# Delta rule: a head's outputs are computed behind the next head's key products, its query products become fillers of the first two levels, and values are projected first

## The reference, cut to what matters

```python
mixed = causal_conv4(hidden @ qkv_w.T)            # 4 taps per channel
q, k, v = split(mixed, 3)                         # 8 heads of 128 each
z = hidden @ z_w.T
beta = sigmoid(hidden @ b_w.T)
alpha = exp(-exp(A_log) * softplus(hidden @ a_w.T + dt_bias))
def step(S, q_t, k_t, v_t, beta_t, alpha_t):      # over the 256 tokens
    S = S * alpha_t
    kv = k_t @ S
    S = S + outer(k_t, (v_t - kv) * beta_t)
    return S, q_t @ S
o = scan(step)
o = o * rsqrt(mean(o * o) + eps) * norm_w         # per head
out = (o * silu(z)) @ out_w.T                     # summed over heads
```

## Time and profile before

| | us |
|---|---|
| median of 3 runs | 4471.35 (4461.21 to 4476.52) |
| the profiled execution | 4470.14 |
| its span (first to last instruction) | 4468.4 |
| of it, heads 1 to 6 of the delta rule | 591.40 |
| PE busy in these | 533.42 |
| DVE, ACT, POOL busy in these | 326.79, 253.91, 147.82 |

### The profile page before, as it was taken

How to read it: one execution, slowest core, us unless ns; L and a number is a source line. 1 busy time by engine, 2 the same in 40 slices (tenths; PEclk the granted TensorE clock), 3 DMA queues, 4 the chain that set the end, 5 groups by cost and what they waited for, 6 DMA issues and landing times. The chain is left out here.

```text
span 4468.4 us, 119856 instructions
## 1 busy us (share of the span) xinstructions
PE 3704.9 (83%) x48264; PEld 2804.5 (63%) x48456; DVE 2663.5 (60%) x4159; ACT 2214.2 (50%) x4350; POOL 1676.8 (38%) x1564
## 2 busy tenths in 40 slices
PE   4666759989989989988988986999999765667998
PEld 1223448868868868867867874666667752225555
DVE  5985567547637727726736736455556255894554
ACT  4443247657647747746756753344444314441222
POOL 1652047527617707716725732222222202661000
PEclk7988979999999999999999997677778777997999
DMA  0000011101101101101101100000000000001000
GB/s 14 0 0 16 1 45 33 38 22 33 42 17 33 40 19 33 31 21 41 32 25 37 31 14 6 6 6 6 7 6 7 4 12 0 0 0 57 0 0 9
DMA packets 56555, 83.31 MB, mean 19 GB/s; under 512 B 13146, under 2 KB 32628, under 8 KB 54900
## 3 DMA queue, kind: packets, MB, share of 16 engines
q1 hardware_dynamic: 56052, 75.99, 5.7%
HBM read 30.87 MB, written 1.05 MB: 7 GB/s over the span
## 5 line engine op out<-in xcount | busy, mean ns | idle before, releaser
L1814 POOL TENSOR_TENSOR local_rot<-local_term 128x512 f32<-128x512 f32 x384 | 478.7, 1268 | 639.3 <-DVE local_term L2132 639.3
L2132 DVE TENSOR_TENSOR local_term<-bank,local_table 128x512 f32<-128x512 f32 x768 | 484.7, 673 | 107.2 <-ACT local_sq L2020 98.7
L2055 ACT ACTIVATE local_attn<-bank 64x256 f32<-64x256 f32 x768 | 290.8, 379 | 338.7 <-PE bank L1911 331.9
L272 POOL TENSOR_TENSOR mamba_hc<-mamba_state,mamba_c_all 128x512 f32<-128x512 f32 x256 | 319.6, 1270 | 318.0 <-DVE mamba_state L451 311.5
L1820 POOL TENSOR_TENSOR local_rot<-local_rot,local_inv 128x512 f32<-128x512 f32 x384 | 392.4, 1043 | 92.5 <-ACT local_inv L2031 91.1
L1855 PE MATMUL bank<-local_w_layer,local_xs 128*128 128x256 f32 x1536 | 400.8, 406 | 24.8 <-issue 17.7
L1855 PEld LDWEIGHTS bank<-local_w_layer,local_xs 128*128 128x128 f32 x1536 | 287.8, 197 | 78.5 <-issue 28.4
L2193 DVE TENSOR_REDUCE local_most<-bank 128x8 f32<-128x512 f32 x192 | 132.8, 692 | 307.8 <-PE bank L1890 307.8
L1911 PE MATMUL bank<-local_pt,local_v_moved 64*128 64x64 f32 x3072 | 314.3, 282 | 0.0
L1911 PE MATMUL bank<-local_pt,local_v_at 64*128 64x64 f32 x3072 | 305.2, 276 | 0.0
L451 DVE TENSOR_TENSOR_SCAN mamba_state<-bank,mamba_dbu 128x512 f32<-128x512 f32 x256 | 297.9, 1203 | 0.0
(11 more groups left out here) (367 smaller groups left out, 8268.7 us busy)
## 6 DMA issues: line engine op xcount, KB each, us to landing
local_v_moved<-local_v_at SPq DMA_DIRECT2D x192, 192.0 KB, 2.4
local_w_layer<-a_w_layer_dram SPq DMA_DIRECT2D x6, 1536.0 KB, 7.3
local_v_moved<-local_v_at SPq DMA_DIRECT2D x192, 32.0 KB, 2.0
moe_w<-f_w_dram SPq DMA_DIRECT2D x3, 2048.0 KB, 15.8
local_w_o<-a_w_o_dram SPq DMA_DIRECT2D x12, 256.0 KB, 3.7
local_w_up<-a_w_up_dram SPq DMA_DIRECT2D x6, 341.0 KB, 4.2
moe_w<-f_w_dram SPq DMA_DIRECT2D x3, 576.0 KB, 5.2
delta_w_h<-g_w_qkv_dram SPq DMA_DIRECT2D x8, 192.0 KB, 2.2
```

The source lines that it names most:

```text
L272: ins = pool.tensor_tensor(hc[:, b, h, :], state[:, b, h, :], c_all[:, b, :], ALU.mult)
L1814: pool.tensor_tensor(rot[:, i % 2, :, f, :], here[:, :, f, :], there[:, :, 1 - f, :], ALU.add).then_inc(summed, 1)
L2055: ins = act.activation(tokens[ch, v, :, :].rearrange("p k (r q) -> p k r q", r=2), g.bank[6 + v][ch, :].rearrange("p (k r h q) -> p k r h ...
L2132: dve.tensor_tensor(term[:, which, b, :], g.bank[b][:, :], table[:, which, :, :].rearrange("p n c -> p (n c)"), ALU.mult).then_inc(roped, 1)
```

## The change

- The output products of head h leave the end of head h. Three quads stand in head h+1 behind its key products and between its first products, the fourth in slot 0 (letter u). Only head 7's stand behind its own head.
- Their squares (ACT), sums (DVE), logarithm, exponential and scaling move with them (letter n, slot 1).
- The query products leave the front of the head for slots 2 to 5 (letter q), with their multiplication on DVE.
- Values are turned in slots 1 to 3, keys in slots 4 and 5, two quads at once, in banks 2 and 3.
- Projections come two slots later at first (p0 in slot 6, before in slot 4), and in the order values, keys, queries.
- `w_sol` gets a buffer of its own, as `lt` is written anew while the outputs are still to be computed.

```diff
-    PROJ, STEPS, ORDER = 3 * GROUPS, TAPS - 1, (1, 0, 2)
+    PROJ, STEPS, ORDER = 3 * GROUPS, TAPS - 1, (2, 1, 0)
...
-        w_sol, o_sq, sz = lt, o_t, g.xn
+        w_sol = sb("w_sol", [P, QUADS, QUAD, C])
+        o_sq, sz = o_t, g.xn
...
-        AT_SLOT = {0: "v0 v1", 1: "k0 k1", 2: "v2 v3", 3: "k2 k3", 4: "p0", 5: "a0", 6: "p1", 7: "a1", 8: "p2", 9: "a2",
+        AT_SLOT = {0: "u3", 1: "v0 v1 n0", 2: "q0 v2", 3: "q1 v3", 4: "q2 k0", 5: "q3 k1", 6: "p0", 7: "a0 p1", 8: "p2",
...
+                if later(h):
+                    pool.wait_ge(o_ready, h * QUADS)
...
+            def weigh_output(h, n):
+                if n == 0:
+                    pe.wait_ge(sz_ready, h * QUADS + QUADS)
+                pe.wait_ge(w_copied, h * (2 * QUADS) + (QUADS + n + 1))
+                for i in range(QUAD):
+                    mm = pe.matmul(chunk(g.bank[4 + n], i), at[:, n, i, :], w_sol[:, n, i, :], start=True, stop=(i < SEQS))
+                    if i >= SEQS:
+                        mm = pe.matmul(chunk(g.bank[4 + n], i), kq_g[:, 0, SEQS * n + i - SEQS, :], s_one[:, n, i - SEQS, :],
+                                       start=False, stop=True)
+                mm.then_inc(o_ready, 1)
...
-                pe.wait_ge(conv_step, h * (PROJ * STEPS) + GROUPS * STEPS)
+                pe.wait_ge(conv_step, h * (PROJ * STEPS) + 2 * GROUPS * STEPS)
                 for n in range(QUADS):
+                    if later(h):
+                        pe.wait_ge(w_copied, h * (2 * QUADS) - (QUADS - 1 - n))
                     four(g.bank[n], lambda i: seg(1, n, i), lambda i: seg(1, n, i), kk_ready)
-                pe.wait_ge(conv_step, h * (PROJ * STEPS) + PROJ * STEPS)
                 pe.wait_ge(a_copied, h * QUADS + QUADS)
-                queries_by_keys(0)
-                queries_by_keys(1)
+                if later(h):
+                    pe.wait_ge(conv_step, h * (PROJ * STEPS) + PROJ * STEPS)
+                    weigh_output(h - 1, 0)
                 first_products(0)
-                queries_by_keys(2)
+                if later(h):
+                    weigh_output(h - 1, 1)
                 first_products(1)
-                queries_by_keys(3)
+                if later(h):
+                    weigh_output(h - 1, 2)
...
+                    if later(h) and hf == 0:
+                        square_output(h - 1, 0)
+                if later(h):
+                    square_output(h - 1, 1)
+                    square_output(h - 1, 2)
```

## The result

The changed kernel takes 4512.81 us (median of 4 runs, 4509.47 to 4525.85) against 4467.19 for the kernel before in the same comparison: a ratio of 1.0101 (95% interval 1.0077 to 1.0126). It is slower by 45.6 us in the medians (45 by the ratio) and by 39.3 in the two profiled executions (4509.47 and 4470.14). The forecast was 4498.

A forecast was written before the change was run, and what follows sets the result against it. PE was taken as the bound: its work at the granted clock plus pauses, a 256-instruction packet taking at least 3.8 us. 4470.1 + 20.5 (five branch-entered heads at +4.1) - 4.5 + 12 = 4498; range 4450 to 4522.

The forecast's parts named there:

- Branch, +3.2: Loop branch into heads 2 to 6: PE waits for two instruction packets, idle 4.8 against 1.6 us, +3.2 each.
- Tail, -5.1: End of a head: output products leave, one projection comes later, a turned output earlier; other waits unchanged; -5.1 us.
- Front, +6.0: Start of heads entered by the branch: +3.6 us with waits for POOL and q0, 2.4 for key products' clock.
- Clock in the levels, +12: Levels: packets with two projections exceed 3.8 us at half clock; +2 us a head, +12 in all.
- Others, -4.5: Heads entered without the branch: heads 1 and 7 -1.5 us each, head 0 -1.5 from two query quads leaving.
- A: Rival: the packet boundary behind the branch costs nothing, idle stays 1.6, clock isn't lost; 4470 us, chance 0.20.
- B: Rival: output and query products keep the clock at 1.0 through the levels; faster, 4446 us, chance 0.17.
- C: Rival: clock falls at the branch, returns only in the last level; up to +9 a head, 4540 us, chance 0.09.

The follow-up runs named there:

- aligned_square: aligned with ACT's square of the first output quad moved behind the second packing instead of between the packings: 4471.9 us, ratio 1.0018.
- 161 and 250 left: Changed kernel padded with extra PE instructions so the loop body starts 161 or 250 instructions ahead of a packet boundary: 4486.1 and 4504.6 us.
- aligned: Changed kernel, loop body 161 instructions ahead of a packet boundary, extra instructions put where PE waits anyway: 4479.8 us, ratio 1.0035.
- b_left2: Kernel before, order untouched, padded so its loop body starts 2 instructions ahead of a boundary instead of 161: 4502.8 us, ratio 1.0093.
- a_left63: Changed kernel padded with extra PE instructions so the loop body starts 63 instructions ahead of a packet boundary: 4512.0 us, ratio 1.0103.
- aligned_order: aligned with padding spread, the square behind the second packing and the last two output projections each ahead of a projection in their slots: 4449.0 us, ratio 0.9971.

## Why the prediction was nearly right

**Branch, +3.2.** Right in kind: a target 2 instructions ahead of a boundary costs two packets, 3.0 apart, as in the earlier trace rows. Measured +4.0 a branch (5.6 instead of 1.6). I let the target's packet move 1.2 before PE is done, as before; in the change it moves 0.25 before. The last products now wait for DVE's last subtraction, and in all five heads the branch begins 0.16 after that has ended, so it comes up later.

**Tail, -5.1.** The work went, as computed. The sentence "the rest of the tail waits as before" is the step that failed. The two waits for DVE's add, 1.25 and 0.77 before (1.24 and 0.77 in the head shown), became one of 2.53, long enough for the clock to fall; with the clock, PE's work in last stretch and tail together falls by 1.0 a head instead of the 4.4 that left it (39 records fewer). Together the two stretches, without the branch, are 0.5 a head shorter, not 5.1. I had listed what moved on PE and not how long DVE needs to its add, and so not that PE's work beside it shrinks by half.

**Front, +6.0.** Measured: +3.6 up to the levels' first product, of it 1.0 for POOL (1.1 expected from ACT's square; in aligned_square this wait is gone) and 1.4 to 2.8 of the key products' clock (2.4 taken). The rest of the 6.0, such as q0's wait of 1.13 for ACT's scaling, doesn't show in the sum: front and levels together are 4.5 longer, and with the 2.0 for the clock I had given them 8.0.

**Clock in the levels, +12.** The levels are 0.9 a head longer, 4.9 over heads 1 to 6, although the clock in them is higher than before (0.74 on average, before 0.62). Another 1.3 a head is in the last stretch behind them, beyond the 2.5 of work that came there; its clock is 0.83 instead of 0.88. That the two add up to about 12 is luck. What I named beside the clock, two packets with two projections each, was a cost, and the runs show it as part of the 3.5 a head between 161 and 250 left.

**Others, -4.5.** Head 0 and the step to head 1 (from the first product with `delta_w_ab` to head 1's first key product) take 141.5 instead of 144.5, 3.0 less where I had computed 6.6. This can't be judged from single profiles: aligned and aligned_square run the same instructions there and take 130.4 and 139.4. The tail ahead of head 7, which has no branch, is 4.8 shorter. Heads 1 and 7 lose 3.4 and 3.8 in the last stretch, where I had counted none (2.5 of it in head 1 is work that came there from the tail).

**Rivals.** A (the boundary costs nothing) falls by b_left2 alone, which is slower with no change of order. B (fillers keep the clock up) had a true premise, the clock in the levels rose, and a price that did not come: the levels got longer, not shorter. The price was not baseless. In the kernel before, the levels of heads 1 to 6 last 53.4 at a clock of 0.56 and 48.8 at 0.65, so there the clock did matter, and the rest of the difference between the earlier trace rows's heads lies in the last stretch (16.6 to 20.0). C did not occur: the clock comes back within 3.4 to 6.8 us.

**The sum.** It came out 15 low (4498 against 4512.8) because large errors nearly cancel. Over heads 1 to 6 last stretch and tail cost some 28 more than forecast and the five branches 4, while front and levels cost 22 less. That leaves 9 of the 11 by which the profiled execution (4509.5) lies above the forecast. The branch, which decided between the forecast and its rivals, was understood; that the total is this near is in part luck.

## What to carry to other kernels

In a program that is bound by its instructions' arrival, shifting code moves every packet boundary behind it: count where a loop's target and the heavy instructions fall before you judge a new order, since here that was 29 to 40 of 45 us. If a wait is for an engine's small result, list what this engine has ahead of it and what the waiting engine has to do meanwhile, and look for the second waiter before moving it; a wait removed in one place came back 5 us later. A stretch whose length doesn't follow its work is the place for fillers, and the order paid (16 us below the kernel before) only once the tail kept its clock and the target its packet.

## What the runs showed of the hardware

- A met wait costs PE's queue 0.11 us an instruction: 97 of them 10.4 us, 159 17.4, 195 21.2, where 64 records of products of 32x32 take 0.74 together. As padding they belong where the engine waits anyway.
- The packets behind a branch overlap with work as soon as the first has something to run. With 63 instructions left, the packets moved at 3096.25 and 3099.25, and the 32 key products ran through from 3098.90 in 3.83 us without a stop; with 2 left nothing runs until 2.6 behind the second. By the Trainium skill, page "Runtime: NRT & Kernel Launch", section "Instruction fetch mechanics", crossing a block is mostly hidden; that agrees with 63, 161 and 250 left behind the branch (idle once, 2.4 to 2.9), and not with 2 left (4.6 to 6.0) or with the levels (a stop of 2.10 in the earlier trace rows).
- The wait of 2.53 in the tail lets the clock fall in all six heads of each of the eight kernels that have it: the output projection behind it takes 1.78 to 2.08 instead of 1.16. The wait of 2.4 to 2.9 at the branch does so in some heads only, and what happened in the tail goes with it. Seven of the eight have 63, 161 or 250 left, which makes 35 such branches. Behind the 11 tails with a mean clock of 0.80 or 0.81 the key products took 3.83, at full clock, and behind the 24 with 0.89 or 0.90 they took 5.46, with one exception (3.83 in head 5 of a_left63). So a long stay at half clock in the tail goes with none at the branch; why is not shown. In aligned_order the tail stays at full clock, and the key products take 5.42 to 5.46 in all five heads.
- The clock is one thing that spreads the executions of a kernel: head 0, the same instructions in aligned and aligned_square, takes 130.4 us at a mean clock of 0.74 in one profile and 139.4 at 0.67 in the other. Why the clock differs there was not tested.
